# Three late steps of a two-layer pre-norm kernel, moved together: index compares and half of the last norm into the last products, and a low-rank product to the join of h

## The chip, the cores and the metric

One core of one Trainium2 chip. The metric is device time in microseconds (us) for one launch of the whole program; the kernel before took 828.55, 828.6 and 832.93 us in three runs, median 828.6.

## The reference

x is [1024, 512] in fp32 and goes through four residual blocks, each with a layer norm ahead of it: a linear layer under a block mask, an int4 linear layer, an NF4 block with low-rank adapters (q, k, v, o, then gate, up, silu, down with 1792 hidden channels), and a feed-forward in simulated NVFP4. The change touches the end of the third block and the whole of the fourth, which is this:

```python
def nvfp4_qdq(x, select_num):
    s = jnp.maximum(jnp.max(jnp.abs(x)) / (448.0 * 6.0), 1e-12)
    xb = (x / s).reshape(x.shape[:-1] + (D // BLOCK, BLOCK))
    sb = jnp.clip(jnp.max(jnp.abs(xb), axis=-1, keepdims=True) / 6.0, 1e-12, 448.0)
    a = xb / sb
    q = jnp.sign(a) * FP4_LEVELS[jnp.digitize(jnp.abs(a), FP4_BOUNDS)]
    dq = (q * sb).reshape(x.shape) * s
    ...   # the last select_num channels stay as they are
xq = nvfp4_qdq(x2[:, up_reorder_index], SEL_UP)
wg = nvfp4_qdq(w_gate[:, up_reorder_index], SEL_UP)
wu = nvfp4_qdq(w_up[:, up_reorder_index], SEL_UP)
h = jax.nn.silu(xq @ wg.T) * (xq @ wu.T)
hq = nvfp4_qdq(h[:, down_reorder_index], SEL_DOWN)
wd = nvfp4_qdq(w_down[:, down_reorder_index], SEL_DOWN)
out = hq @ wd.T * mlp_output_scale
out = out + x2 @ lr_A @ lr_B
```

The scale s is a maximum over the whole tensor, once of x and once of h (1024 x 1376). So there are two points where nothing that needs the quantised values can begin before everything ahead is done. They are called the join of x and the join of h here.

## The kernel before, in words

Tokens lie on the 128 partitions in 8 tiles of 128 (n = 0 to 7), channels in 4 groups of 128 (k). A product in fp32 precision is three matmuls of 512 columns, high by high, low by high and high by low, at lines 1141, 1142 and 1143 (`pass3`); high and low parts are made by a cast on ACT and a subtraction on DVE or POOL.

`make_plan()` (line 271 on) writes one list of steps with `p.add`. Five functions (`pe_program`, `act_program`, `dve_program`, `pool_program`, `sp_program`) walk this list, and each issues what its engine has to do for a step. So the order of `p.add` is the order on every engine, and an engine that waits holds all its later steps. `p.take` gives a result a bank of PSUM from a ring, with the step that frees it. In the fourth block both rings have four banks (`main4`: banks 0, 1, 2, 7; `turn4`: the other four).

The stages from the end of the third block on, with the steps that the change touches:

- Last products of the third block. Gate/up product and down product for group 6, second token half (`("gu", 6, 1)` with four parts and `("d", 6, 1)` with tiles 4 to 7; the order is set by `order` at line 655). Ahead of `("d", 6, 0)`, four products earlier, stands the step `perm`: SP loads the order of the channels, and DVE turns it to float (L1933) and compares it against the channel numbers in four instructions (L1936). The result is a matrix of zeros and ones by which a product permutes channels. Each down product is added to x on DVE (`dn_add`, L1928). The hidden values of a part come from ACT and, as a product with its high part, from POOL (`gu_mul`).
- Last norm (`norm_turn(3)`, L512): per tile BN_STATS and its kin on DVE, the normed tile `ztok` on ACT, four transposes on PE (`turn`, L1291), the high part from ACT (`tsplit`), the low part from DVE (`tdiff`, L1762). It begins once two down products of the second half have been issued, tile 0 ahead of the last two.
- Permuted product (`pprod`, L1395 on, one matmul pass by the zeros and ones per tile), taken off PSUM by `ptake`. At the same time PE turns weight rows that are gathered by GpSimd in an indirect DMA (`rowfetch`, `rowturn`, `rowsplit`).
- Join of x: `low_a(0)`, `low_a(1)`, the first low-rank product (x by A, 64 wide), around `greatest_of_all("x")`: transposes of the maxima (L1403), a reduce, and a broadcast back (L1407). `low_take` takes x by A off PSUM with ACT (L1608) and DVE (L1962).
- Quantisation of x: `round`, `scale`, `qturn` (transposes, L1437), and between them the hidden product of the first 352 channels, `hidden(0)`, and the second low-rank product: `low_b(n)` for 8 tiles, three matmuls each from 64 partitions, in banks of `main4`, each added to x by DVE (`low_add`, L1967, 8 times). `fetch_pair(1)` turns the next weight rows.
- Hidden products 1 and 2, with `hmm` on PE and silu on ACT. `pair_vacant(1)` (L1205) holds the first load into the buffers of the second pair until `low_b(7)` is done.
- Join of h: `hmax`, `greatest_of_all("h")`: PE transposes the maxima (L1403), DVE reduces, PE broadcasts (L1407), DVE computes the scale (`floor`, `rec`, L2012 on) and rounds the first tile (L2023 to L2036), and PE turns it (L1437).
- Last stage: rounding, turning and the down product of h, tile by tile; `fin` (L2055) adds it to x and the tile goes out.

Of the kernel before, what the change touches and what calls it, by code (L numbers as in the profile page):

```python
# [16 lines left out]
P = 128  # L17
# [27 lines left out]
MASK_LOWS = 2  # L45
MORE_HOTS = 24
# [95 lines left out]
HN = NT // 2  # L142
SCALED_AT = {(0, 0): (0, 1), (0, 2): (1, HN), (HN - 1, 0): (HN, NT)}
# [127 lines left out]
def make_plan():  # L271
# [240 lines left out]
    def norm_turn(ln):  # L512
        norm(ln, 0)
# [6 lines left out]
        for n in range(NT):  # L520
# [132 lines left out]
    norm4, normed = norm_turn(3), 2  # L653
# [39 lines left out]
    for what, g, half in order:  # L693
# [7 lines left out]
        for i, _ in enumerate((gate_up if what == "gu" else down)(g, half)):  # L701
            side_nf4.step()
            side_fp4.step()
            if (what, g, half, i) == ("d", NG - 1, 1, 1):
                next(norm4)
        through.add((what, g, half))
        if (what, g, half) == ("gu", NG - 1, 1):
            next(norm4)
# [7 lines left out]
    def norm4_rest():  # L716
        for n in range(normed):
            yield n
        yield from norm4
        yield None  # L720
        yield None
# [14 lines left out]
    def greatest_of_all(what):  # L736
# [5 lines left out]
        else:  # L742
            p.add("rec", "h", 2, 1)
        p.add("allone", what)
# [8 lines left out]

    for step, _ in enumerate(permuted()):
# [11 lines left out]
    def low_rank():  # L766

        p.add("low_take", 1)
        yield
        for n in range(0, NT + 2, 2):  # L770
            for m in range(n - 2, n):
                if m >= 0:
                    p.add("low_add", m)
            for m in range(n, min(n + 2, NT)):
                p.add("low_b", m)
                main4(("lb", m), ("dve", "low_add", m))
            yield
# [4 lines left out]
    p.add("scale", "x", 0, NT)  # L782

    def turned_tiles(items):
# [50 lines left out]
    first_hidden, low, second = hidden(0), low_rank(), fetch_pair(1)  # L835
    for step, _ in enumerate(turned_tiles([("x", n, 0) for n in range(NT)])):
        if step >= 2:
            next(low, None)
            next(first_hidden, None)
        if step == 3 or step >= 7:  # L840
# [23 lines left out]
    weave(hidden(2), Side(itertools.chain.from_iterable(map(down_rows, range(3))), 1.75))  # L864
    p.add("hmax")
    greatest_of_all("h")
    due = []
# [48 lines left out]
def build(nc, a, out, ctx):  # L916
# [70 lines left out]
    with ExitStack() as late:  # L987
# [8 lines left out]
        w_last = sb("w4_h", [P, 1, 512], F32R, late), sb("w4_l", [P, 1, 512], F32R, late)  # L996

# [24 lines left out]
    lt = [[v[0:LR, 2 + half, :] for v in lrs] for half in range(2)]  # L1022
# [1313 lines left out]
```

## Time and profile before

| | |
|---|---|
| runs | 828.55, 828.6, 832.93 us; median 828.6 |
| profiled execution | 826.45 us, its span 825.0 us |
| granted TensorE clock, mean | 0.958 |
| instructions | 11310 |
| busy PE, DVE, ACT, POOL | 726.9, 570.4, 442.3, 188.5 us |

The profile is of one execution, which was 2.15 us shorter than the median of the three runs. Busy shares are of the whole span. The stages above lie at these times from the start of the span: last products up to 545 us, permuted product up to 572, join of x 572 to 579, quantisation of x and hidden(0) 579 to 650, hidden 1 and 2 up to 732, join of h 732 to 743, last stage 743 to 825. In a row of the timeline the first number is the start, the second the time that the group took; a bracket holds the idle time of the engine ahead of it and what ended it.

### The profile page before, as it was taken

What the parts mean: (1) busy time and instruction counts of PE and PEld (TensorE: products, weight loads), DVE (VectorE), ACT (ScalarE), POOL (GpSimd) and SP (SyncE); (2) the same over time, 40 slices, a digit from 0 to 9 for tenths busy, and PEclk for the clock granted to TensorE, in tenths of its full rate; (3) what the DMA queues carried; (4) which work ended last, traced back from release to release, by engine and by line L of the source; (5) the groups of instructions that cost most, each with busy time, mean ns of one, the idle gap of its engine ahead of it and who ended that gap; (6) DMA issues with size and microseconds to landing.
All of it is one profiled execution on the core that took longest, in us unless ns stands there. A gap on an engine that the chain in (4) does not pass through costs nothing.

```text
span 825.0 us, 11310 instructions
## 1 busy us (share of the span) xinstructions
PE 726.9 (88%) x4136; PEld 540.4 (66%) x4136; DVE 570.4 (69%) x1087; ACT 442.3 (54%) x573; POOL 188.5 (23%) x174
## 2 busy tenths in 40 slices
PE   1898765979999998889998998788899899959998
PEld 1665523656767766557665777566677688957886
DVE  5779967662688778789897985468463433567773
ACT  4778777564876868677766612255422221224542
POOL 1013000004253462435544444112301100000000
PEclk9999968999999999999998999999999999989999
DMA  8636678766376686647655112101301110200001
GB/s 292 213 120 215 198 256 277 254 201 215 129 224 214 201 241 204 236 143 265 232 180 163 65 38 57 42 27 43 99 0 36 36 51 1 87 1 14 25 27 39
DMA packets 56087, 110.55 MB, mean 134 GB/s; under 512 B 9936, under 2 KB 20848, under 8 KB 56032
## 3 DMA queue, kind: packets, MB, share of 16 engines
q1 hardware_dynamic: 42912, 79.22, 29.3%
q10 hardware_dynamic: 8736, 16.52, 6.2%
q0 software_dynamic: 4384, 14.09, 5.6%
q8 instruction: 33, 0.54, 0.3%
q14 instruction: 22, 0.18, 0.1%
HBM read 91.65 MB, written 18.15 MB: 133 GB/s over the span
## 4 chain that ended last, share of the span: by engine, by line
PE 55%; DVE 21%; issue 8%; ACT 8%; DMA 5%; SPq 1%; ACTq 1%; POOL 0%; DVEq 0%; POOLq 0%
PE bank L1141 14%; PE bank L1142 13%; PE bank L1143 13%; PE bank L1249 3%; ACT hot L1551 2%; DVE hot L1805 2%; DMA wide_buf<-in_down_flat 2%; DVE x L1928 2%; PE bank L1437 2%; ACT c L1510 2%; DVE q_a L1878 2%; DVE bank L1831 2%; DVE q_r L1872 1%; PE bank L1291 1%; PE bank L1262 1%
## 5 line engine op out<-in xcount | busy, mean ns | idle before, releaser
L1551 ACT ACTIVATE hot<-rep,levels 128x2048 f16<-128x2048 f16 x96 | 193.6, 2057 | 14.9 <-ACT c L1510 12.1
L1141 PE MATMUL bank<-zt_h,w_h 128*128 128x512 f32 (+1 forms) x232 | 95.1, 410 | 2.6 <-DVE zt_l L1916 2.0
L1142 PE MATMUL bank<-zt_l,w_h 128*128 128x512 f32 (+1 forms) x232 | 92.8, 400 | 0.0
L1143 PE MATMUL bank<-zt_h,w_l 128*128 128x512 f32 (+1 forms) x232 | 92.5, 399 | 0.0
L1249 PE MATMUL bank<-hot,diag 128*32 128x512 f16 x1160 | 78.1, 399 | 2.3 <-ACT hot L1551 2.2
L1141 PE MATMUL bank<-w_h,xq_h 128*128 128x512 f32 (+1 forms) x192 | 74.3, 387 | 5.2 <-DVE w_l L1947 3.0
L1142 PE MATMUL bank<-w_l,xq_h 128*128 128x512 f32 (+1 forms) x192 | 72.3, 376 | 0.0
L1143 PE MATMUL bank<-w_h,xq_l 128*128 128x512 f32 (+1 forms) x192 | 72.2, 376 | 0.0
L2072 POOL TENSOR_TENSOR q_a<-q_a,q_m 128x384 f32<-128x384 f32 (+3 forms) x34 | 35.7, 1049 | 107.9 <-DVE q_m L1691 107.8
L1249 PEld LDWEIGHTS bank<-hot,diag 128*32 128x32 f16 x1160 | 26.1, 98 | 44.9 <-issue 22.8
L2128 POOL TENSOR_TENSOR at_l<-ztok,at_h 128x512 fp32r<-128x512 f32 x28 | 37.5, 1341 | 76.1 <-ACT at_h L1583 76.1
L1141 PE MATMUL bank<-w_h,at_h 128*128 128x512 f32 x112 | 47.9, 427 | 7.2 <-DVE x L1928 5.6
L1141 PEld LDWEIGHTS bank<-zt_h,w_h 128*128 128x128 f32 (+1 forms) x232 | 44.6, 192 | 12.7 <-DVE zt_l L1916 2.4
L2044 DVE TENSOR_TENSOR hid<-hid,bank 128x512 f32<-128x512 f32 (+1 forms) x24 | 15.1, 628 | 53.5 <-PE bank L1143 29.9
L1143 PEld LDWEIGHTS bank<-zt_h,w_l 128*128 128x128 f32 (+1 forms) x232 | 44.6, 192 | 10.5
L1805 DVE TENSOR_SCALAR hot<-rep,levels 128x2048 f16<-128x2048 f16 x58 | 51.0, 879 | 0.1
L1142 PEld LDWEIGHTS bank<-zt_l,w_h 128*128 128x128 f32 (+1 forms) x232 | 44.7, 193 | 9.4
L1583 ACT CAST at_h<-ztok 128x512 fp32r<-128x512 f32 x28 | 17.3, 619 | 60.6 <-DVE ztok L1923 60.6
L1843 DVE TENSOR_TENSOR w_l<-bank,w_h 128x512 fp32r<-128x512 f32 x46 | 31.6, 687 | 24.3 <-ACT w_h L1559 24.0
L1141 PEld LDWEIGHTS bank<-w_h,xq_h 128*128 128x128 f32 x192 | 36.9, 192 | 13.5 <-DVE w_l L1947 3.4
L1142 PE MATMUL bank<-w_l,at_h 128*128 128x512 f32 x112 | 45.4, 405 | 0.0
L1143 PE MATMUL bank<-w_h,at_l 128*128 128x512 f32 x112 | 45.2, 404 | 0.0
(224 smaller groups left out, 1682.7 us busy)
## 6 DMA issues: line engine op xcount, KB each, us to landing
rep<-codes SPq DMA_DIRECT2D x58, 512.0 KB, 4.2
codes<-c SPq DMA_DIRECT2D x28, 256.0 KB
raw<-in_codes_gu_t ACTq DMA_DIRECT2D x14, 512.0 KB, 5.0
sc<-in_scales_gu_t SPq DMA_DIRECT2D x56, 128.0 KB, 4.3
raw<-in_codes_attn_t ACTq DMA_DIRECT2D x8, 512.0 KB, 4.0
raw<-in_codes_down_t ACTq DMA_DIRECT2D x7, 512.0 KB, 5.0
sc<-in_scales_down_t SPq DMA_DIRECT2D x28, 128.0 KB, 3.0
wide_buf<-in_gate_flat SPq DMA_DIRECT2D x5, 512.0 KB, 4.5
```

The costliest lines, as they stand in the source:

```text
L1141: PE.matmul(psum, lh, rh, start=first, stop=False, **kw)
L1142: PE.matmul(psum, lh, rl, start=False, stop=False, **kw)
L1143: return PE.matmul(psum, ll, rh, start=False, stop=last, **kw)
L1249: mm = PE.matmul(bank[32 * q:32 * q + 32, :], lhs, hots[plan.slot[hot_ring(t), (t, m)]][:, q, :], start=m == LOOK_ORDER[0] and part == 0, ...
L1437: last = PE.matmul(bank[0:nr, tok(t)], slot[:, t * P:t * P + nr], ident, start=t == 0, stop=False, is_transpose=True, skip_group_check=True)
L1510: S.copy(c16[:], raw[:]).then_inc(sem("cast_act"), 1)
L1551: S.activation(hots[plan.slot[hot_ring(t), (t, m)]][:], codes_in_place(t), ACT.Relu, bias=bias, scale=slope).then_inc(sem("ramp_act"), 1)
L1583: S.copy(hs[half][0][:, f, :], ztok[plan.slot["ztok", ("silu", *key)]][:]).then_inc(sem("gu_mul_act"), 1)
L1805: ins = V.tensor_scalar(hot, codes_in_place(t), levels[:, HITS:HITS + 1], levels[:, HIT_VALUE:HIT_VALUE + 1], ALU.is_equal, ALU.mult)
L1843: V.tensor_tensor(wl[:, k, :], look_bank(t)[:], wh[:, k, :], ALU.subtract).then_inc(sem("made_dve"), 1)
L2072: G.tensor_tensor(ua[:, 0:nq], ua[:, 0:nq], um[:, 0:nq], ALU.add).then_inc(own.sem, 1)
L2128: G.tensor_tensor(hs[half][1][:, f, :], ztok[plan.slot["ztok", ("silu", *key)]][:], hs[half][0][:, f, :], ALU.subtract).then_inc(sem("gu_m ...
```

## The change

Five things at once, all by moving steps in the plan:

1. The DVE work of `perm` becomes a step `permute` of its own. The loads stay where they were; the cast and the four compares come after the first gate/up part of `("gu", 6, 1)`.
2. The first half of the last norm (tiles 0 to 3) is spread over the eight parts of `("gu", 6, 1)` and `("d", 6, 1)` by `norm4_early`. Tiles 4 to 7 follow after it.
3. The down products of tiles 4, 5 and 6 are cut in two. `dn_ahead` puts their first three matmuls (first 128 of 256 hidden channels) ahead of all of them, and `dn_mm` does the other three.
4. The product `low_b` goes from the quantisation of x to the join of h: tiles 0 and 1 ahead of `greatest_of_all("h")`, 2 and 3 within it, 4 to 7 behind it. Four of its banks come from `turn4`. The addition to x is no longer on DVE: ACT copies the bank to a new buffer `low_sum` and POOL adds it to x. ACT's copies for tiles 6, 7, 4 and 5 stand behind the first rounding of h.
5. `low_take(1)`, and the split of B (a new step `lr_b`, on ACT and POOL), come right after the scale at the join of x, ahead of the first rounding. Their result lies in other buffers, so `pair_vacant(1)` waits for `low_a(1)` only, and `fetch_pair(1)` turns rows from step 5 on instead of step 7.

The core of the diff:

```diff
     def down(g, half):
         for n in range(4 * half, 4 * half + 4):
-            p.add("dn_mm", g, n)
-            p.take("main", 3, ("dn", g, n), ("dve", "dn_add", g, n))
+            if (g, n) in AHEAD:          # AHEAD = (6, 4), (6, 5), (6, 6)
+                if (g, n) == AHEAD[0]:
+                    for ahead in AHEAD:
+                        p.add("dn_ahead", *ahead)
+                        p.take("main", 3, ("dn", *ahead), ("dve", "dn_add", *ahead))
+                p.add("dn_mm", g, n)
...
+    def norm4_early(what, i):
+
+        if (what, i) == ("gu", 0):
+            p.add("permute")
+        elif (what, i) == ("gu", 1):
+            norm(3, 0)
+        elif (what, i) == ("gu", 2):
+            turn_early(0)
+            norm(3, 1)
+        elif (what, i) == ("gu", 3):
+            turn_early(1)
+            split_early(0)
+        elif (what, i) == ("d", 0):
+            split_early(1)
+            norm(3, 2)
+        elif (what, i) == ("d", 1):
+            turn_early(2)
+            norm(3, 3)
+        elif (what, i) == ("d", 2):
+            turn_early(3)
+            split_early(2)
+        else:
+            split_early(3)
...
     p.add("scale", "x", 0, NT)
+    p.add("low_take", 1)
+    p.add("lr_b")
...
-        if step == 3 or step >= 7:
+        if step == 3 or step >= 5:
             next(second)
...
         if c == 1:
-            return [done("pe", "pprod", NT - 1), done("pe", "low_b", NT - 1)]
+            return [done("pe", "low_a", 1)]
...
             p.add("rec", "h", 2, 1)
+            low_b(2, 3)
+            for n in range(4):
+                p.add("low_add", n)
...
                 p.add("round", *item)
+                if item == ("h", 0, 0):
+                    for n in LATER_ADDS:     # 6, 7, 4, 5
+                        p.add("low_add", n)
...
+    low_b(0, 1)
     p.add("hmax")
     greatest_of_all("h")
+    low_b(4, 5, 6, 7)
...
+            elif kind == "dn_ahead":
+                g, n = key
+                half = n // HN
+                bank, (hh, hl), (wh, wl) = main(("dn", *key)), hs[half], wring[2]
+                pe.wait_ge(*done("pool", "gu_mul", g, half, 0))
+                pe.wait_ge(*done("dve", "made", 2 * last_of["down", g] + 1))
+                for m in vacant("main", ("dn", *key)):
+                    pe.wait_ge(*m)
+                k0, tc = 2 * (g % 2), tok(n % HN)
+                pass3(bank[:], hh[:, 0, tc], hl[:, 0, tc], wh[:, k0, :], wl[:, k0, :], True, False)
...
+            elif kind == "low_add":          # ACT
+                n, = key
+                act.wait_ge(*done("pe", "low_b", n))
+                S.copy(low_sum[:, n, :], low_bank(n)[:]).then_inc(sem("low_add_act"), 1)
...
-            elif kind == "low_add":          # DVE
-                n, = key
-                dve.wait_ge(*done("pe", "low_b", n))
-                V.tensor_tensor(x[:, n, :], x[:, n, :], main4(("lb", n))[:], ALU.add).then_inc(sem("low_add_dve"), 1)
...
+            elif kind == "low_add":          # POOL
+                n, = key
+                pool.wait_ge(*done("act", "low_add", n))
+                G.tensor_tensor(x[:, n, :], x[:, n, :], low_sum[:, n, :], ALU.add).then_inc(sem("low_add_pool"), 1)
```

DVE's queue where the index compares stood, before. The rows are line, operation, output and inputs; the first TENSOR_TENSOR adds a down product to x, `hid` here holds the indices, `xq_l` the matrix of zeros and ones.

```order
L1928 TENSOR_TENSOR x<-x,bank2 128x512
L1843 TENSOR_TENSOR w2_l<-bank5,w2_h 128x512
L1933 CAST hid<-hid 128x512
L1936 TENSOR_SCALAR xq_l<-hid,channel 128x512 x4
L1928 TENSOR_TENSOR x<-x,bank0 128x512
L1727 BN_STATS stats<-x 128x6
```

The same place after; the cast and the compares now stand behind the norm's small work, ahead of the first addition to `ztok0`.

```order
L1995 TENSOR_TENSOR x<-x,bank2 128x512
L1910 TENSOR_TENSOR w2_l<-bank5,w2_h 128x512
L1995 TENSOR_TENSOR x<-x,bank0 128x512
L1794 BN_STATS stats<-x 128x6
...
L1822 SCALAR_TENSOR_TENSOR mv<-mv,inv_dev 128x4
L2000 CAST hid<-hid 128x512
L2003 TENSOR_SCALAR xq_l<-hid,channel 128x512 x4
L1990 TENSOR_TENSOR ztok0<-ztok0,bank2 128x512
```

So the additions of group 6 to x no longer stand behind the cast and the compares, and these stand behind the first norm statistics.

DVE's queue at the join of x before: the scales, then at once the first rounding (`q_a0` and `q_a1` are two tiles of it).

```order
L2012 TENSOR_SCALAR rec<-rec,gm4 128x8x24
L2023 TENSOR_TENSOR q_a0<-hid,rec 128x384
L2023 TENSOR_TENSOR q_a1<-hid,rec 128x384
L2030 SCALAR_TENSOR_TENSOR q_a0<-q_m0,q_a0 128x384
```

After, the low part of x by A (`zt_l` from its bank) stands between them.

```order
L2075 TENSOR_SCALAR rec<-rec,gm4 128x8x24
L2029 TENSOR_TENSOR zt_l<-bank1,zt_h 64x512
L2086 TENSOR_TENSOR q_a0<-hid,rec 128x384
L2086 TENSOR_TENSOR q_a1<-hid,rec 128x384
L2093 SCALAR_TENSOR_TENSOR q_a0<-q_m0,q_a0 128x384
```

TensorE's queue at the join of h before: the transpose of the maxima, the broadcast, and the transposes of the first rounded tile (`q_d0`).

```order
L1143 MATMUL bank1<-w1_h,xq_l 128x352
L1403 MATMUL bank3<-ident_r,gm4 1x128
L1407 MATMUL bank3<-ident_r,row 128x1
L1437 MATMUL bank5<-ident_r,q_d0 128x128 x4
```

After, the eight tiles of the second low-rank product, three matmuls each, stand ahead of, between and behind the two.

```order
L1193 MATMUL bank1<-w1_h,xq_l 128x352
L1191 MATMUL bank2<-zt_h 128x512
L1192 MATMUL bank2<-zt_l,zt_h 128x512
L1193 MATMUL bank2<-zt_h,zt_l 128x512
...
L1463 MATMUL bank3<-ident_r,gm4 1x128
L1191 MATMUL bank4<-zt_h 128x512
...
L1467 MATMUL bank3<-ident_r,row 128x1
L1191 MATMUL bank0<-zt_h 128x512
...
L1193 MATMUL bank3<-zt_h,zt_l 128x512
L1497 MATMUL bank4<-ident_r,q_d0 128x128 x4
```

Two tiles lie ahead of the transpose of the maxima, two ahead of the broadcast and four ahead of the first turned tile of h.

## Rows read from the trace of the kernel before

**Rows 1.** The page: busy time, share of the span and instructions of each engine.
```profile
PE 726.9 (88%) x4136; PEld 540.4 (66%) x4136; DVE 570.4 (69%) x1087; ACT 442.3 (54%) x573; POOL 188.5 (23%) x174
```

**Rows 2.** Windows: stretch, length, busy PE, PEld, DVE, ACT, POOL, clock, DMA, GB/s.
```profile
520.00:533.50 13.50, 13.50 (x53) 10.69 (x51) 6.12 (x19) 3.31 (x5) 1.29 (x1) 0.87 0.00 1
533.50:545.60 12.10, 8.94 (x38) 6.83 (x37) 6.08 (x10) 4.51 (x7) 1.27 (x1) 0.86 0.01 1
579.00:650.00 71.00, 65.59 (x295) 51.09 (x295) 35.90 (x60) 21.93 (x44) 10.80 (x12) 0.98 0.15 45
732.00:743.30 11.30, 2.40 (x7) 1.22 (x8) 10.28 (x27) 2.68 (x6) 0.00 (x0) 0.67 0.00 1
```

**Rows 3.** Timeline at the index compares: start, time, engine, line, operation, [idle, releaser].
```profile
516.56 0.43 DVE L1933 CAST hid<-hid 128x512 f32<-128x512 int32 x1 [5.05 <-DMA hid<-in_up_idx]
...
518.61 0.68 DVE L1928 TENSOR_TENSOR x<-x,bank 128x512 f32<-128x512 f32 x1
...
519.35 0.50 PE L1141 MATMUL bank<-w_h,at_h 128*128 128x512 f32 x1 [3.31 <-DVE x L1928]
```

**Rows 4.** Timeline, last down products to the permuted product.
```profile
533.12 0.39 PE L1143 MATMUL bank<-zt_h,w_l 128*128 128x512 f32 x1
...
535.03 1.27 POOL L2128 TENSOR_TENSOR at_l<-ztok,at_h 128x512 fp32r<-128x512 f32 x1 [4.14 <-ACT at_h L1583]
...
543.00 0.39 PE L1143 MATMUL bank<-w_h,at_l 128*128 128x512 f32 x1
...
543.23 0.40 PE L1141 MATMUL bank<-w_h,at_h 128*128 128x512 f32 x1
...
545.54 0.50 PE L1395 MATMUL bank<-xq_l,zt_h 128*128 128x512 f32 x1
...
552.67 0.52 PE L1291 MATMUL bank<-ident_r,ztok 128*128 128x128 f32 x3 [1.83 <-DVE zt_l L1762]
```

**Rows 5.** Timeline at the join of x.
```profile
573.80 1.03 DVE L2023 TENSOR_TENSOR q_a<-hid,rec 128x384 f32<-128x384 f32 x2
...
574.71 0.40 PE L1143 MATMUL bank<-zt_h,w_l 128*64 128x512 f32 x1
...
574.95 0.56 DVE L2030 SCALAR_TENSOR_TENSOR q_a<-q_m,q_a 128x384 f32<-128x384 bf16 x1
...
581.23 0.68 DVE L1962 TENSOR_TENSOR w_l<-bank,w_h 64x512 fp32r<-64x512 f32 x1 [2.30 <-ACT w_h L1608]
```

**Rows 6.** Timeline of the quantisation of x and its end.
```profile
587.33 0.50 PE L1141 MATMUL bank<-w_h 64*128 64x512 f32 x1
...
590.12 0.47 PE L1141 MATMUL bank<-w_h,xq_h 128*128 128x512 f32 x1 [1.14 <-ACT hid L1650]
...
620.98 0.50 PE L1141 MATMUL bank<-w_h,xq_h 128*128 128x512 f32 x1 [0.24 <-ACT xq_l L1636]
...
650.02 0.50 PE L1141 MATMUL bank<-w_h,xq_h 128*128 128x512 f32 x1 [2.95 <-DVE w_l L1947]
...
652.38 0.63 PE L1141 MATMUL bank<-w_h,xq_h 128*128 128x512 f32 x1
...
652.81 0.63 PE L1142 MATMUL bank<-w_l,xq_h 128*128 128x512 f32 x1
```

**Rows 7.** Timeline of PE at the join of h.
```profile
733.55 0.27 PE L1403 MATMUL bank<-ident_r,gm 128*1 128x128 f32 x1 [1.71 <-DVE gm L1978]
...
735.21 0.22 PE L1407 MATMUL bank<-ident_r,row 1*128 1x1 f32 x1 [1.39 <-DVE row L1996]
...
740.29 0.69 PE L1437 MATMUL bank<-ident_r,q_d 128*128 128x128 f32 x2 [4.87 <-DVE q_d L2036]
```

**Rows 8.** POOL and DVE side by side at 505 us, and all of DVE's line 1677.
```profile
505.10 1.29 POOL L2128 TENSOR_TENSOR at_l<-ztok,at_h 128x512 fp32r<-128x512 f32 x1 [3.44 <-ACT at_h L1583]
505.25 1.17 DVE L1677 TENSOR_SCALAR q_r<-q_r 128x14 f32<-128x14 f32 x1
...
L1677 DVE TENSOR_SCALAR q_r<-q_r x34: 174/179/1172, 209.8 to 505.3; 128x24 f32<-128x24 f32 x20, 128x32 f32<-128x32 f32 x8, 128x14 f32<-128x14 f32 x4, 96x24 f32<-96x24 f32 x2
```

More of the change, by code:

```diff
@@ L142 @@
 HN = NT // 2
+AHEAD = tuple((NG - 1, n) for n in range(HN, HN + 3))
 SCALED_AT = {(0, 0): (0, 1), (0, 2): (1, HN), (HN - 1, 0): (HN, NT)}
@@ L510, in norm, with norm_turn @@
         p.take("ztok", 2, ("norm", ln, n), ("pe", "turn", ln, n))
-    def norm_turn(ln):
-        norm(ln, 0)
+    def norm_turn(ln, first=0):
+        if not first:
+            norm(ln, 0)
         if ln == 0:
@@ L519, in norm_turn @@
         turned = None
-        for n in range(NT):
+        for n in range(first, NT):
             p.add("turn", ln, n)
@@ L643, in down @@
         for n in range(4 * half, 4 * half + 4):
-            p.add("dn_mm", g, n)
-            p.take("main", 3, ("dn", g, n), ("dve", "dn_add", g, n))
+            if (g, n) in AHEAD:
[5 more added lines that the diff above has]
+            else:
+                p.add("dn_mm", g, n)
+                p.take("main", 3, ("dn", g, n), ("dve", "dn_add", g, n))
             yield
@@ L651, in down, with turn_early, split_early @@
                     known(3, 0)
-    norm4, normed = norm_turn(3), 2
+    def turn_early(n):
+        p.add("turn", 3, n)
+        turn_bank(("ln", 3, n), split_done(3, n))
+    def split_early(n):
+        p.add("tsplit", 3, n)
+        p.add("tdiff", 3, n)
+    def norm4_early(what, i):
[18 more added lines that the diff above has]
+            split_early(2)
+        else:
+            split_early(3)
     side_nf4, side_fp4 = Side(ready_nf4, NF4_RATE), Side(fp4, FP4_RATE)
@@ L703, in make_plan @@
             side_fp4.step()
-            if (what, g, half, i) == ("d", NG - 1, 1, 1):
-                next(norm4)
+            if (g, half) == (NG - 1, 1):
+                norm4_early(what, i)
         through.add((what, g, half))
-        if (what, g, half) == ("gu", NG - 1, 1):
-            next(norm4)
     p.turn4 = p.turns % 2
@@ L716, in norm4_rest @@
     def norm4_rest():
-        for n in range(normed):
-            yield n
-        yield from norm4
+        yield from range(HN)
+        yield None
+        yield from norm_turn(3, HN)
         yield None
@@ L752, in turn_bank @@
         turn4(key, *freed_by)
+    norm(3, HN)
     for step, _ in enumerate(permuted()):
@@ L764, in low_a, with low_b @@
         main4(("la", half), ("dve", "low_take", half))
[L766 to L777, printed above, removed]
+    def low_b(*tiles):
+        for n in tiles:
+            p.add("low_b", n)
+            (turn4 if n in LOW_IN_TURNS else main4)(("lb", n), ("act", "low_add", n))
     low_a(0)
@@ L833, in hidden @@
         p.note("hup", c, due)
-    first_hidden, low, second = hidden(0), low_rank(), fetch_pair(1)
+    first_hidden, second = hidden(0), fetch_pair(1)
     for step, _ in enumerate(turned_tiles([("x", n, 0) for n in range(NT)])):
         if step >= 2:
-            next(low, None)
             next(first_hidden, None)
-        if step == 3 or step >= 7:
+        if step == 3 or step >= 5:
             next(second)
@@ L996, in build @@
         w_last = sb("w4_h", [P, 1, 512], F32R, late), sb("w4_l", [P, 1, 512], F32R, late)
+    with ExitStack() as end:
+        low_sum = sb("low_sum", [P, NT, D], F32, end)
     wraw = wide_buf[:].rearrange("p (k n) -> p k n", k=KD)
@@ L1021, in build @@
     lrs = w_more
-    lt = [[v[0:LR, 2 + half, :] for v in lrs] for half in range(2)]
+    lt = [[z[0:LR, half * D:half * D + D] for z in zt_flat] for half in range(2)]
+    lr_b = [z[0:LR, 2 * D:3 * D] for z in zt_flat]
     gm4_of = {"x": gm4[:, 0:1], "h": gm4[:, 1:2]}
@@ L1039, in main4, with low_bank @@
         return banks[(0, 1, 2, 7)[plan.slot["main4", key]]]
+    def low_bank(n):
+        return turn(("lb", n)) if n in LOW_IN_TURNS else main4(("lb", n))
     def turn_vacant(key):
@@ L1364, in pe_program @@
                 k0, tc = 2 * (g % 2), tok(n % HN)
-                for k in range(2):
+                for k in range(1 if key in AHEAD else 0, 2):
                     last = pass3(bank[:], hh[:, k, tc], hl[:, k, tc], wh[:, k0 + k, :], wl[:, k0 + k, :], k == 0,
```

36 lines of the change are left out of this document (22 added, 14 removed).

## The prediction

> **What bounds the kernel now.** I read the page first: PE is busy 88% of the span and no other engine is above 69% [rows 1]. So a change can win by taking PE's idle time or slow clock, and hardly by taking work from DVE, ACT or POOL. Then I read windows over the stages that the change touches, for PE's busy time and clock [rows 2]. PE is packed in the x quantisation (65.59 of 71.00 us). At the join of h it works 2.40 of 11.30 us while DVE works 10.28, so DVE bounds there. In the two stretches around the last products the clock is 0.87 and 0.86, where the page's mean is 0.958. Last I read the timeline at each PE gap for what ends it [rows 3 to 7]. Sums are made against the profiled execution, 826.45 us (span 825.0); that run was 2.15 under the median of 828.6, and I add this back at the end.
>
> One price first. Products are issued one matmul after the other: 543.00 to 543.23 is 0.23 us a matmul at the full clock of 2.4 GHz [rows 4], and 652.38 to 652.81 is 0.43 at the lower level of 1.2 GHz [rows 6].
>
> **A, the index compares leave the first-half down products.** DVE waits 5.05 us for the indices, until 516.56; the cast, the compares and one addition follow, and PE stands 3.31 us for that addition [rows 3]. After the move nothing on DVE waits for the indices at this place, and at the new place, some 10 us later, they have landed. PE gets back 3.3. After the gap the stretch up to 533.5 runs at clock 0.87 [rows 2]: 13.50 us x 0.13 = 1.75 lost, which I read as the price of the pause and count as won. A = -5.1 (bounds -3.3, if the clock dips anyway, and -5.1).
>
> **B, last norm and split products.** The last gate/up matmul starts at 533.12, the first permuted one at 545.54 [rows 4]: 12.4 us, in which PE is busy 8.94 of 12.10 [rows 2]. The largest pause is for POOL's product of hidden values (535.03 + 1.27 = 536.30, after 4.14 us without work) [rows 4]. After the change this stretch holds a turn (0.55), nine matmuls ahead (9 x 0.23 = 2.1) that need only the first half of the hidden values, a wait for the rest, 15 more matmuls (3.5) and two to three turns (1.4); with the wait at 0.5 that is 8.1. B = 8.1 - 12.4 = -4.3, of which 0.2 is uncertain either way. If DVE or ACT cannot serve norm and hidden values at once, half is lost: bounds -2 and -5.
>
> **C, permuted product.** The gap of 1.83 for the low part of a turned tile [rows 4] goes, since tiles 0 to 3 are ready; the same engines make tiles 4 to 7 in the same time, so I let new waits of 0.7 appear. C = -1.1 (bounds 0 and -1.8).
>
> **D, join of x.** Now DVE goes from the scales straight to the first rounding at 573.80, while PE still does `low_a(1)` until 574.71 + 0.40 = 575.11 [rows 5]. After the change DVE first takes x by A off PSUM, which waits for that product and ACT's copy (0.6, an estimate from the 0.56 and 0.68 of the rows beside it), and takes 0.68 itself [rows 5]: 575.11 + 0.6 + 0.68 - 573.80 = +2.6 ahead of everything that waits for the first rounding. Beside that, POOL's subtraction for B runs at the same moment as DVE's first rounding. What that does, the trace has elsewhere: at 505.25 a DVE instruction of 14 columns takes 1.17 us where the median of its line is 179 ns, while POOL works from 505.10 to 506.39 [rows 8]: it ends as POOL ends. So I add 1.1. D = +3.7 (bounds +2.6, +4.0).
>
> The Trainium skill has the rule for this (SBUF — State Buffer, "Who interferes with whom"): the two engines share ports by a lock that blocks the second to ask, for instructions with two SBUF inputs and in fast modes; the trace agrees, with 1.17 us against 179 ns. By the rule D is +3.7, and without it +2.6; it speaks against F below too.
>
> **E, quantisation of x.** 24 matmuls of `low_b` leave a stage where PE is packed [rows 2]; one stands at 587.33 [rows 6]. 24 x 0.233 = 5.6. The products before and after them wait little now, and some waits that they covered come up, as the 0.24 at 620.98 [rows 6]; I take four of 0.3, +1.2. The gap of 1.14 at 590.12 goes, as the additions to x leave DVE. The last gap of 2.95 at 650.02 stands ahead of the second hidden product, which waits for weight rows that DVE has split [rows 6]; these now start two steps earlier, and I count it all. After it the clock falls, 652.38 on, for about 4 us: 0.20 more a matmul, 1.4 to 1.8. Sum: -5.6 + 1.2 - 1.1 - 3.0 - 1.5 = -10.0 (bounds: -4.4 if nothing but the matmuls comes, -11.5 without new waits).
>
> **F, join of h.** PE has three gaps there, 1.71, 1.39 and 4.87 [rows 7], together 8.0, and the 24 matmuls need 5.6 at full clock, so they fit; the window's clock is 0.67 [rows 2], and at 0.43 a matmul 24 take 10.3. The first two tiles stand ahead of the transpose of the maxima, 1.4 to 2.6, against a gap of 1.71; so up to 0.9 late. ACT's copies fit in its 8.6 us idle. What does not fit is POOL. DVE bounds the join with short operations on SBUF; no POOL work is there now (0.00) [rows 2]. Eight additions with two SBUF inputs come, each about the 1.29 of the POOL row at 505.10 [rows 8]: 10.3 us in two batches of four. If every DVE instruction gets its turn only between two of POOL's, the first batch is in series: 4 x 1.29 = 5.2. Of the second, DVE is one tile ahead and PE has products queued, so I take half less 0.8: 1.8. F = +7.0 (bounds: -1 if POOL does not disturb and the slow clock ends earlier, +11.6 if all eight and one more wait are in series).
>
> **Sum.** -5.1 - 4.3 - 1.1 + 3.7 - 10.0 + 7.0 = -9.8. 826.45 - 9.8 = 816.65 profiled; with 2.15, 818.8.
>
> **Rivals.**
>
> R1: POOL hardly disturbs DVE, because most instructions of the join are small or read PSUM. For it: of the 34 instructions of that DVE line the median stays at 179 ns, so most met no harm. Against it: the one that fell on POOL's work took 1.17 us [rows 8]. Then F = 0 and D = +2.6: 826.45 - 5.1 - 4.3 - 1.1 + 2.6 - 10.0 = 808.55, with 2.15 810.7. Chance 0.15.
>
> R2: the early parts win half. PE's gaps are moved, not filled: in B, ACT and DVE, which have their queues in a fixed order, do the norm ahead of hidden values, and in E the stage turns from PE to the loop of rounding, turning and splitting. For it: DVE works 35.90 us and ACT 21.93 of 71.00 there [rows 2], with long dependent chains. Against it: PE is packed 92%, so little of the loop shows. Then B, C, E give -2.2, -0.5, -5.0: 826.45 - 5.1 - 7.7 + 3.7 + 7.0 = 824.35, with 2.15 826.5. Chance 0.15.
>
> R3, slower: the low clock outlives the join of h. The join grows by 7 and is emptier in part, the clock there is 0.67 [rows 2], and a matmul at the lower level costs 0.20 more [rows 6]. Each us of the last stage at 1.2 GHz loses half a us. If it stays for 28 us, 14 are lost: 818.8 + 14 = 832.8. It decides from about 20 us (10 lost, all the gain). For it: after the pauses at 519 and 650 the clock dips [rows 2, 6]. Against it: after the gap at 650.02 it was low for about 4 us only, and the low-rank product now keeps PE busier in the join. Chance 0.05.
>
> R4: the change does not do what it says: the first tiles of `low_b` at the low clock delay the maxima by up to 2.3 and everything of the join behind them. That is 818.8 + 2.3 = 821.1, inside my range; chance 0.1.
>
> **How the numbers follow.** Forecast 818.8, chance 0.55; its own range 815 to 823. R1 0.15, R2 0.15, R4 0.10, R3 0.05. To hold 8 in 10 the range goes down to 808.5, which leaves out the far side of R1, and up to 826.5, the middle of R2, which leaves out R3 and half of R2. What a measurement can tell from no change is 0.5%, 4.1 us: faster is under 824.5, slower over 832.7. Faster: forecast, R1, R4 and a third of R2, 0.85. Same: the rest of R2, 0.10. Slower: R3, 0.05.
>
> **What the new profile would show.** A: no PE gap by an addition to x in the first-half products, clock over 0.95 there. B: the first permuted matmul 4 us sooner after the last gate/up one than 12.4. D: the first rounding about 2.6 us later behind the scales, with one subtraction of DVE in between, and the first rounding above its usual 1.03 for two. E: no `low_b` between 579 and 650, the stage 8 to 10 us shorter, gaps under 1 ahead of the second hidden product. F: eight POOL additions at the join, DVE's rounding instructions over 1 us each where they were 0.5, and the first turned tile of h 5 us later behind the maxima. If those instructions keep their time, my F is wrong and the time is near 811; if PE waits as long as before in the x stage, R2 holds.

## The result: less than half of the gain that was forecast

| | before | after |
|---|---|---|
| runs, median | 828.55 to 832.93, 830.15 us (8 runs) | 824.32 to 826.47, 825.64 us (8 runs) |
| profiled execution | 826.45 us | 826.44 us |
| span, mean clock | 825.0 us, 0.958 | 825.0 us, 0.948 |

The ratio is 0.994 (95% interval 0.9927 to 0.9954), a gain of 4.5 us by the medians. The forecast was 818.8 with -9.8: the time lies inside the range of 808.5 to 826.5, but the gain is less than half of the one forecast.

The two profiled executions show no difference at all, and that is the first thing to clear up. In both, PE does the same matmuls up to the gap at 519 us. The 2731st of them starts at 502.05 before and at 506.42 after, though nothing that the change touches lies ahead of it. Over all profiles of this study that start lies between 500.67 and 510.75 us, in code that is the same. Much of this goes with the chip: it is 505.12 to 506.87 in the four experiments on chip 4, 507.21 to 510.75 on chip 13 and 500.67 to 504.51 on chip 7. (For the two kernels here the chip is not on record.) The profiled execution of before was faster than all eight timed runs. From that matmul on the two profiles differ by -4.4, which is what the medians show.

So every profile is read from that matmul on, in stages whose borders are starts of matmuls in PE's timeline: the last one of the gate/up product (533.12 before), the first permuted one (545.54), the transpose of the maxima of x (570.99), the first turned tile of x (576.75), the last hidden matmul (731.52), the fifth transpose of h (743.30), and the end. The stages are the steps A to F of the prediction, with A ending at the gate/up product.

| change of each stage, us | A | B | C | D | E | F | rest | sum |
|---|---|---|---|---|---|---|---|---|
| forecast | -5.1 | -4.3 | -1.1 | +3.7 | -10.0 | +7.0 | 0 | -9.8 |
| after | -4.7 | -4.5 | +5.6 | +3.4 | -10.9 | +5.9 | +0.7 | -4.4 |

Five of six terms are within 1.1 us. C missed by 6.7.

The profile after. The page's busy times stand as those of before do in [rows 1]: PE as before, POOL 11 us more.

```profile
PE 728.5 (88%) x4136; PEld 541.1 (66%) x4136; DVE 572.7 (69%) x1079; ACT 447.7 (54%) x581; POOL 199.9 (24%) x182
```

Windows of after, columns as in [rows 2]: the permuted stage, the quantisation of x, the join of h.

```profile
540.70:571.76 31.06, 26.15 (x125) 20.79 (x125) 19.68 (x42) 15.14 (x27) 5.49 (x6) 0.89 0.16 43
580.97:644.96 63.99, 61.05 (x277) 47.76 (x277) 30.10 (x52) 22.59 (x46) 12.34 (x13) 0.96 0.19 55
726.89:745.00 18.11, 11.76 (x33) 8.13 (x34) 17.08 (x27) 7.73 (x15) 10.66 (x8) 0.58 0.00 1
```

The permuted stage took 25.45 us before (545.54 to 570.99) and takes 31.06 now. PE is busy for 26.15 of it and stands for the other 4.9 us, in two gaps of 1.40 and 3.50. The join of h has 10.66 us of POOL where it had none, and DVE is busy 17.08 of 18.11.

**Where C went.** Timeline of PE in the permuted stage of after. L1341 is the turn of a normed tile, L1445 that of weight rows, L1455 the permuted product.

```profile
550.00 0.60 PE L1341 MATMUL bank<-ident_r,ztok 128*128 128x128 f32 x4
552.01 0.66 PE L1341 MATMUL bank<-ident_r,ztok 128*128 128x128 f32 x4 [1.40 <-ACT ztok L1581]
552.50 0.60 PE L1445 MATMUL bank<-ident_r,hid 128*128 128x128 f32 x4
556.60 1.09 PE L1341 MATMUL bank<-ident_r,ztok 128*128 128x128 f32 x4 [3.50 <-DVE w_l L2014]
557.34 0.78 PE L1455 MATMUL bank<-xq_l,zt_h 128*128 128x512 f32 x1
557.92 0.63 PE L1456 MATMUL bank<-xq_l,zt_l 128*128 128x512 f32 x1
```

Tiles 4 and 5 are turned, then PE stands 3.50 us for a bank of PSUM that DVE's split of weight rows (L2014) frees. Behind the waiting turn of tile 6 stands the permuted product of tile 4 (L1455 and L1456). DVE in the same stretch:

```profile
553.16 0.69 DVE L1829 TENSOR_TENSOR zt_l<-bank,zt_h 128x512 fp32r<-128x512 f32 x1 [0.95 <-ACT zt_h L1588]
553.77 0.68 DVE L2020 TENSOR_REDUCE blk<-bank 128x32 f32<-128x512 f32 x1
...
554.73 0.75 DVE L1742 RECIPROCAL rec<-rec 128x96 f32<-128x96 f32 x1
...
555.77 0.69 DVE L2014 TENSOR_TENSOR w_l<-bank,w_h 128x512 fp32r<-128x512 f32 x1
```

The low part of tile 4 (L1829) is there at 553.85, 2.75 us before PE moves on. The product had its inputs; it was queued behind a turn that could not run. Before the change the first-half products filled this time. Now they are done by 550, and nothing covers the second half's chain. It starts on ACT:

```profile
544.35 1.28 ACT L1574 ACT_TABLE_LOAD   x1 [4.47 <-DVE mv L1806]
...
547.22 0.82 ACT L1581 ACTIVATE ztok<-x,mv,inv_dev 128x512 f32<-128x512 f32 x1 [1.36 <-DVE mv L1822]
547.94 0.57 ACT L1671 COPY hid<-bank 128x512 f32<-128x512 f32 x1
```

ACT waits 4.47 us for the statistics, with the takes of permuted tiles (L1671) behind. I first took this for the main cause. After the gap the granted clock is at its lower level (a permuted matmul 0.63 us long where 0.40 is usual, as at 557.92) until 562.4. So the +5.6 can be taken apart: 4.90 us of gaps where before had 1.83, +3.1; from 556.60 to 562.4 PE works at the lower level, 5.8 us, by an estimate from 0.43 a matmul against 0.23 about +2.8; one turn fewer lies in the stage, about -0.35.

**D and F.** At the join of x in after, first the wait that was forecast, then POOL and DVE side by side:

```profile
575.46 0.40 PE L1193 MATMUL bank<-zt_h,w_l 128*64 128x512 f32 x1
575.89 0.58 ACT L1675 CAST zt_h<-bank 64x512 fp32r<-64x512 f32 x1 [3.35 <-PE bank L1193]
...
576.57 0.68 DVE L2029 TENSOR_TENSOR zt_l<-bank,zt_h 64x512 fp32r<-64x512 f32 x1 [2.06 <-ACT zt_h L1675]
577.07 1.78 POOL L2201 TENSOR_TENSOR zt_l<-hid,zt_h 64x512 fp32r<-64x512 f32 x1 [22.74 <-ACT zt_h L1653]
577.18 2.08 DVE L2086 TENSOR_TENSOR q_a<-hid,rec 128x384 f32<-128x384 f32 x2
```

The two multiplications took 1.03 before [rows 5] and take 2.08. The join of h, POOL and DVE, in after:

```profile
727.72 0.43 DVE L1744 TENSOR_SCALAR rec<-rec 128x88 f32<-128x88 f32 x1
...
728.50 0.91 DVE L2059 COPY row<-row 1x127 f32<-1x127 f32 x1
...
730.49 1.37 DVE L2074 TENSOR_SCALAR blk<-blk,gm 128x86 f32<-128x86 f32 x1
...
734.45 5.76 POOL L2205 TENSOR_TENSOR x<-x,low_sum 128x512 f32<-128x512 f32 x4 [2.67 <-ACT low_sum L1657]
734.90 1.63 DVE L2099 TENSOR_TENSOR q_d<-q_a,blk 128x512 f32<-128x512 f32 x1
736.46 1.36 DVE L2074 TENSOR_SCALAR blk<-blk,gm 128x258 f32<-128x258 f32 x1
737.74 1.35 DVE L2075 TENSOR_SCALAR rec<-rec,gm 128x258 f32<-128x258 f32 x1
739.13 1.33 DVE L2086 TENSOR_TENSOR q_a<-hid,rec 128x224 f32<-128x224 f32 x1
```

POOL's four additions of the row run from 734.45 to 740.22, the second batch. The four DVE instructions that start in that time take 0.9 to 1.0 us longer than in a kernel that has no additions there (f_held, below), 258 columns as much as 512. The first batch runs from 726.77 to 731.79, and there not every DVE instruction is late: the COPY, L1744 and L2074 are, but four instructions of one column between 729.72 and 730.45 take their usual 0.15 to 0.16, and a reciprocal of 88 columns its 0.70. Between the two batches, from 731.8 to 734.45, DVE keeps its pace.

### The profile page after: what moved, and what is told of

It reads as the page before. It is cut to its first block, busy times and chain, and to the rows that moved or that the text cites. A ratio compares the mean times of both kernels' runs of the same rounds, so it can differ in the third digit from the quotient of the medians.

```text
span 825.0 us, 11312 instructions
## 1 busy us (share of the span) xinstructions
PE 728.5 (88%) x4136; PEld 541.1 (66%) x4136; DVE 572.7 (69%) x1079; ACT 447.7 (54%) x581; POOL 199.9 (24%) x182
## 4 chain that ended last, share of the span: by engine, by line
PE 53%; DVE 20%; ACT 10%; issue 9%; DMA 4%; SPq 1%; another core or an unknown queue 1%; ACTq 1%; POOL 0%; DVEq 0%; POOLq 0%
PE bank L1191 13%; PE bank L1192 13%; PE bank L1193 13%; PE bank L1299 3%; ACT hot L1611 3%; DMA wide_buf<-in_down_flat 2%; DVE x L1995 2%; DVE hot L1872 2%; ACT c L1570 2%; DVE bank L1898 2%; PE bank L1497 2%; DVE q_a L1945 1%; PE bank L1312 1%; PE bank L1341 1%; DVE q_r L1939 1%
## 5 line engine op out<-in xcount | busy, mean ns | idle before, releaser
L1193 PEld LDWEIGHTS bank<-zt_h,w_l 128*128 128x128 f32 (+1 forms) x232 | 43.9, 189 | 10.3
L1191 PE MATMUL bank<-w_h,zt_h 128*128 128x512 f32 (+1 forms) x104 | 43.5, 418 | 0.0
```

What stands on the lines that cost most here:

```text
L1191: PE.matmul(psum, lh, rh, start=first, stop=False, **kw)
L1193: return PE.matmul(psum, ll, rh, start=False, stop=last, **kw)
```

## The experiments

Each was timed beside runs of the kernel before on the same chip. Chips differ between rows: chip 4 (before 831.21 us) has a_compares, c_half_late, c_norm_at2 and f_no_adds; chip 13 (832.61) has f_held, d_later, c_product_first and g_all; chip 7 (827.07) has the rest. So ratios are compared, not times, and two ratios that differ by under 0.3% are not told apart. The table has the ratio, and the stages as above of the one profile of each kernel, against the profile of before.

| kernel | ratio (95%) | A | B | C | D | E | F | sum |
|---|---|---|---|---|---|---|---|---|
| a_compares | 0.9966 (0.9953 to 0.9979) | -5.2 | +1.0 | 0.0 | 0.0 | +0.1 | 0.0 | -3.9 |
| c_half_late | 0.9948 (0.9929 to 0.9967) | -5.2 | +1.1 | 0.0 | +3.5 | -10.5 | +6.1 | -4.3 |
| after | 0.994 (0.9927 to 0.9954) | -4.7 | -4.5 | +5.6 | +3.4 | -10.9 | +5.9 | -4.4 |
| c_norm_at2 | 0.994 (0.992 to 0.9959) | -4.7 | -4.5 | +3.2 | +3.6 | -9.7 | +6.0 | -4.9 |
| c_first_only | 0.9909 (0.988 to 0.9938) | -4.7 | -4.5 | +1.0 | +3.6 | -10.3 | +5.9 | -8.0 |
| c_product_first | 0.9886 (0.9861 to 0.9911) | -4.7 | -4.5 | -0.2 | +3.6 | -9.7 | +6.0 | -8.3 |
| f_no_adds | 0.9876 (0.9856 to 0.9896) | -4.7 | -4.5 | +4.1 | +3.6 | -10.1 | +0.1 | -10.9 |
| f_held | 0.9889 (0.986 to 0.9918) | -4.7 | -4.5 | +4.1 | +3.6 | -10.1 | +0.1 | -10.9 |
| d_later | 0.9874 (0.9845 to 0.9903) | -4.7 | -4.5 | +5.7 | 0.0 | -9.5 | +6.0 | -6.9 |
| d_split_later | 0.9946 (0.9924 to 0.9968) | -4.7 | -4.5 | +4.2 | +2.6 | -9.6 | +6.0 | -4.7 |
| e_fetch7 | 1.0004 (0.9979 to 1.0029) | -4.7 | -4.5 | +4.2 | +3.6 | -5.4 | +5.9 | -0.4 |
| g_half_late | 0.9832 (0.9805 to 0.9859) | -5.2 | +1.1 | 0.0 | 0.0 | -10.9 | +0.1 | -14.4 |
| g_all | 0.9778 (0.9753 to 0.9803) | -4.7 | -4.5 | -0.2 | 0.0 | -9.4 | +0.1 | -18.1 |

The sum holds the rest up to the end too, at most 1.3. Sum and ratio agree within 2 us, save for d_later. E lies between -9.4 and -10.9 in all kernels that turn the weight rows early, without order by what was changed, so differences of E under 1.5 are not read.

**a_compares**

```diff
-            p.add("perm")
...
+            if (what, g, half, i) == ("gu", NG - 1, 1, 0):
+                p.add("perm")
```

> The kernel before with part 1 of the change alone: the cast and the four compares of the indices stand behind the first gate/up part of the second half. Theory (parts add up; the profile after shows 5.2 us for this part): 830.15 - 5.2 = 825 us, ratio 0.994. Rival (the clock dip behind the gap comes anyway, only the 3.3 us of the gap are won): 827 us, ratio 0.996.

Measured 828.29 against 831.21, -2.8 us by the ratio. The stage wins 5.2, and 1.0 comes back in B, where the clock was low for 6.8 us (from 533.9) and in the profile before for 3.4. The two other kernels with the compares moved and the late norm, c_half_late and g_half_late, have 6.8 there too. That is three profiles against one, so that the longer dip belongs to the change is likely and not shown. The time fits the rival (827 of 830.15, a ratio of 0.996), though for another reason than it gave: the dip behind the old gap is gone.

**c_half_late**

```diff
-AHEAD = tuple((NG - 1, n) for n in range(HN, HN + 3))
+AHEAD = ()
...
-            if (g, half) == (NG - 1, 1):
-                norm4_early(what, i)
+            if (what, g, half, i) == ("gu", NG - 1, 1, 0):
+                p.add("permute")
+            if (what, g, half, i) == ("d", NG - 1, 1, 1):
+                next(norm4)
...
```

> The kernel after with parts 2 and 3 undone: the last norm's first half and the down products of tiles 4 to 6 stand as before. Theory (the early half wins 4.0 up to the first permuted product and loses 5.6 in the permuted stage, since ACT's takes stand behind the second half's statistics): 1.6 us faster than after, about 824, and in its trace no gap over 2 us of PE in the permuted stage. Rival (the loss in the permuted stage has another cause, such as the gathers or a chance dip of the clock): 4 us slower than after, about 829.5.

Measured 0.9948 where after has 0.994: the same. C falls from +5.6 to 0.0 and B rises from -4.5 to +1.1. So parts 2 and 3 as they stand bring nothing. The theory's 1.6 us faster did not come: by the ratios it is 0.7 slower, by the stages the same. The rival's 4 us slower is excluded.

**c_norm_at2**

```diff
-    norm(3, HN)
     for step, _ in enumerate(permuted()):
+        if step == 2:
+            norm(3, HN)
```

> The kernel after with the second half's statistics and its first normed tile issued after the take of permuted tile 0, not ahead of all takes. Theory (ACT's order is the cause: the takes wait behind the statistics, then ACT has 8.6 us of work at a stretch and PE runs dry): the PE gaps of 1.40 and 3.50 us in the permuted stage shrink by 1.2 to 2.5 together, and the clock dip after them may go; 1.5 to 5 us faster than after, 821 to 824. Rival (gathers or the chain of the second half itself decide): same as after within 0.5 us, or slower by what the statistics are late, 0.5 to 1 us.

Measured 0.994, as after: the time is the rival's. The gap of 1.40 is gone, so the two gaps shrink by 1.2 together, but the other stays, in its PE timeline:

```profile
555.85 0.66 PE L1342 MATMUL bank<-ident_r,ztok 128*128 128x128 f32 x4 [3.69 <-DVE w_l L2015]
```

C is +3.2, where the six kernels with after's order have 4.1 to 5.7. So ACT's order is the small part of the loss. That it was the main cause, my first theory of C, fell here.

**c_product_first and c_first_only.** The first has the statistics' move too, the second only this (`next(rest, "end")` issues the next turn):

```diff
-        for n in norm4_rest():
-            if turned is not None:
+        rest = norm4_rest()
+        while True:
+            early = turned is not None and turned >= HN
+            if early:
+                p.add("pprod", turned)
+                main4(("p", turned), ("dve", "ptake", turned))
+            n = next(rest, "end")
+            if n == "end":
+                return
+            if turned is not None and not early:
                 p.add("pprod", turned)
```

> The kernel after with the statistics of the second half behind the take of tile 0, and, for tiles 4 to 7, the permuted product issued on PE ahead of the next turn and not behind it. Theory (PE stands 3.5 to 3.7 us for a bank, with the permuted product of tile 4 ready but queued behind the turn of tile 6): the gap falls under 1.5 us, the permuted stage is 2 to 4 us shorter than with the statistics moved alone, whose step from the first permuted product to the maxima was 3.2 us longer than before; the time is 2 to 5 us below after, 821 to 823.5. Rival (ACT and DVE are the bound of this stretch, whatever PE's order): the gap moves to the next turn or product and the time is that of after within 1 us.

> The kernel after with PE's order alone changed: for tiles 4 to 7 the permuted product ahead of the next turn; the second half's statistics still ahead of all takes. Theory A (the queued product is the main cause of the 5.6 us, ACT's order a small one): from the first permuted product to the maxima 1 to 1.5 us longer than before, against 4.1 to 5.7 in after and -0.2 with both cures. Theory B (both are needed, as ACT's backlog decides): 3 us or more longer than before.

Measured 0.9886 with both and 0.9909 with this alone; C is -0.2 and +1.0. The timeline of PE in c_first_only (L1463 is the permuted product, L1349 the turn):

```profile
548.72 0.50 PE L1463 MATMUL bank<-xq_l,zt_h 128*128 128x512 f32 x1 [0.81 <-DVE zt_l L1837]
...
551.41 0.63 PE L1349 MATMUL bank<-ident_r,ztok 128*128 128x128 f32 x4 [0.57 <-DVE w_l L2022]
```

The gap of 3.50 has become 0.81 and 0.57 with a product between them, and the clock stays up through the stage. PE's order is the main cause of the miss: 3.1 to 4.7 us of C, of which 2.1 are idle time and the rest goes with the dip of the clock; the order of ACT is another 1.2. Theory A's 1 to 1.5 came out at 1.0, and theory B's 3 or more is excluded. The statistics moved alone (c_norm_at2) take 0.9 to 2.5 off C and nothing off the time.

**f_no_adds and f_held**

```diff
-                G.tensor_tensor(x[:, n, :], x[:, n, :], low_sum[:, n, :], ALU.add).then_inc(sem("low_add_pool"), 1)
+                G.tensor_tensor(low_sum[:, n, 0:1], x[:, n, 0:1], low_sum[:, n, 0:1], ALU.add).then_inc(sem("low_add_pool"), 1)
```

```diff
...
-            elif kind == "low_add":
+            elif kind == "low_sum":
                 n, = key
                 pool.wait_ge(*done("act", "low_add", n))
-                G.tensor_tensor(x[:, n, :], x[:, n, :], low_sum[:, n, :], ALU.add).then_inc(sem("low_add_pool"), 1)
+                pool.wait_ge(*done("pe", "qturn", "h", n, 0 if n else 2))
+                G.tensor_tensor(x[:, n, :], x[:, n, :], low_sum[:, n, :], ALU.add).then_inc(sem("low_sum_pool"), 1)
...
```

The first diff is f_no_adds, the second f_held: there the addition becomes a step of its own, `low_sum`, added to the plan behind the copies, and waits for a transpose of the last stage.

> The kernel after with POOL's eight additions of the low-rank product at the join of h cut to one column each, so the low-rank part is left out of the output. Theory (POOL's additions hold up DVE's short operations at the join): DVE's L2074, L2075, L2086 and L2099 keep their usual 0.3 to 0.7 us there, and the time is 6 to 7 us below after, about 819. Rival (the low-rank matmuls at the low clock, or ACT's copies, delay the join): as after, 825.6, the first turned tile of h as late behind the maxima.

> The kernel after with all of POOL's eight additions kept, but each held back until the last stage: tile 0 until the third piece of tile 0 of h is turned, tile n until the first piece of tile n is. ACT's copies stay at the join. Theory (POOL's additions cost the join 5.9 to 6.6 us, and in the last stage PE bounds and DVE has slack): 5 to 6 us below after, 820 to 821; the join as in the kernel without additions. Rival (a DVE instruction held up by POOL is late for PE in the last stage as well, since the rounding chain is the limit there too): 0 to 2 us below after.

Measured 0.9876 and 0.9889, by the ratios 5.3 and 4.2 us below after, with the same F of +0.1 and sums of -10.9. So all of F was POOL's additions, and in the last stage all eight are free to within the noise. They still hold DVE there: a rounding step at 746.46 takes 1.67 where its neighbours take 0.69, but PE, which has products queued, is not late. DVE at the join in f_held:

```profile
730.11 0.21 DVE L2061 COPY row<-row 1x127 f32<-1x127 f32 x1
...
731.53 0.27 DVE L2076 TENSOR_SCALAR blk<-blk,gm 128x86 f32<-128x86 f32 x1
...
734.85 0.69 DVE L2101 TENSOR_TENSOR q_d<-q_a,blk 128x512 f32<-128x512 f32 x1
735.46 0.35 DVE L2076 TENSOR_SCALAR blk<-blk,gm 128x258 f32<-128x258 f32 x1
735.73 0.35 DVE L2077 TENSOR_SCALAR rec<-rec,gm 128x258 f32<-128x258 f32 x1
736.11 0.39 DVE L2088 TENSOR_TENSOR q_a<-hid,rec 128x224 f32<-128x224 f32 x1
```

The same six took 0.91, 1.37, 1.63, 1.36, 1.35 and 1.33 in after; L1744's 0.43 is 0.21 here. Added up, DVE loses 2.0 us beside the first batch and 3.9 beside the second, together the 5.9 of F. POOL's own time is unchanged in size, 10.7 us for eight:

```profile
L2208 POOL TENSOR_TENSOR x<-x,low_sum 128x512 f32<-128x512 f32 x8 | 10.7, 1335 | 150.8 <-PE bank L1499 150.8
```

**d_later and d_split_later.** Both steps, or `lr_b` alone, issued at step 2 of the quantisation:

```diff
-    p.add("low_take", 1)
-    p.add("lr_b")
...
+        if step == 2:
+            p.add("low_take", 1)
+            p.add("lr_b")
```

> The kernel after with the taking of x by A (second half) and the split of B not ahead of the first rounding of x, but two roundings later. Theory (D as measured, 3.45 us: 2.4 of waiting for PE and ACT in DVE's order, 1.05 of POOL beside the first rounding): the first turned tile of x comes 3.4 us sooner behind the maxima than in after, and the time is 2.5 to 3.5 below after, 822 to 823. Rival (the quantisation of x is bounded by something that starts independently, such as the gathered rows): first turned tile sooner, but the start of hidden product 1 within 0.5 us of after, and so the time.

> The kernel after with the split of B alone (ACT's cast and POOL's subtraction) issued two roundings later; x by A is still taken ahead of the first rounding. Theory (3.45 us is 2.4 of DVE's wait and 1.05 of POOL beside the first rounding): the first two rounding multiplications take 1.03 us and not 2.08, the first turned tile of x comes 1.0 us sooner behind the maxima, with 2.4 left. Rival (the wait is all of it, and DVE only waits longer): 0.3 us sooner or less.

D is 0.0 and +2.6, against +3.4 to +3.6: 1.0 for POOL, 2.6 for the order of DVE, as forecast. In d_split_later the two multiplications take 1.01 again:

```profile
570.44 0.68 DVE L2030 TENSOR_TENSOR zt_l<-bank,zt_h 64x512 fp32r<-64x512 f32 x1 [2.06 <-ACT zt_h L1676]
571.05 1.01 DVE L2087 TENSOR_TENSOR q_a<-hid,rec 128x384 f32<-128x384 f32 x2
```

In the time less can be seen: d_split_later is 0.9946, as after, and 1.0 us is below what these ratios tell apart. In d_later E holds a new gap of PE, 1.50 at 601.03, so part of the 3.4 is given back; g_all, with the same step moved, has 0.53 there and g_half_late none over 0.5. The six runs of d_later spread over 10 us (818.15 to 828.26), so its ratio is weak evidence; its stages are better.

**e_fetch7**

```diff
-        if step == 3 or step >= 5:
+        if step == 3 or step >= 7:
```

> The kernel after with the turning of the second pair of weight rows from step 7 of the quantisation of x again, not from step 5. Theory (the gap of 2.95 us ahead of hidden product 1 goes by the two earlier steps): the gap comes back, 2 to 3 us, with a dip of the clock, +3 to +4 us from the first turned tile of x to the middle of hidden 1 and 2, about 829 us. Rival (the gap went since the rows no longer wait for the low-rank product): within 1 us of after.

Measured 1.0004, no faster than before. In its timeline the gap of 2.95 [rows 6] is back, within 0.01:

```profile
641.87 0.50 PE L1191 MATMUL bank<-w_h,xq_h 128*128 128x512 f32 x1 [2.96 <-DVE w_l L2014]
```

In after the row reads:

```profile
644.96 0.50 PE L1191 MATMUL bank<-w_h,xq_h 128*128 128x512 f32 x1 [0.26 <-DVE w_l L2014]
```

E is -5.4, where the other kernels with the early rows have -9.4 to -10.9: one number in one condition is worth 4.0 to 5.5 us with the clock dip (low for 3.4 us from 642.5), somewhat over the theory's 3 to 4. The rival is excluded. Freeing the load from the low-rank product is worth nothing alone; whether the early rows would pay without it was not run. The -5.4 that is left is the moved product, and F's +5.9 takes all of it. So without the early rows the five-part change wins nothing.

**g_half_late and g_all.** g_all has the cures of f_held, d_later and c_product_first; g_half_late has the first two, with parts 2 and 3 of the change undone.

> The version with the additions held and x by A taken later, but the last norm's first half and the down products as before, that is with parts 2 and 3 of the change undone. Theory (parts 2 and 3 win 5 us once their permuted stage is mended and nothing before): steps of A, E and F as in the version with all cures, 819 us, 5 us above it (814.2). Rival (the mended early half wins little, and the 814.2 come from the two other cures): 815 to 816.

> The three cures together: additions held to the last stage, x by A taken later, statistics behind the first take and products ahead of turns. Theory (all three losses are separate stretches, so the gains add): -5.9 - 3.4 - 3 = 12 us below after, 813.5. Rival (the second stage of a gain is eaten by the clock or the next limit): 816 to 819.

g_all measures 814.16 us (812.99 to 814.84) against 832.61, ratio 0.9778; that beats both kernels, and the gain is about 18 us where the change alone brings 4.5. The gains add, as the theory had it (813.5); the rival's 816 to 819 is excluded. g_half_late is 0.9832, so parts 2 and 3, once mended, are worth the difference of the ratios, 0.54% or 4.5 us, near the theory's 5. By the stages it is 5.3 in A to C and 3.8 in all, as E differs by 1.5 the other way. The two ratios are of different chips, and with their intervals the 4.5 can be 1.5 to 7.5. Parts 2 and 3 were never separated from each other.

## Why the prediction was wrong, step by step

- **A**, forecast -5.1: -5.2 alone, and -4.7 in after, where a turn of the early norm lies in it. The clock's share was booked as won; in a_compares 1.0 comes back in a longer dip at the next pause.
- **B**, forecast -4.3: -4.5. The gap for POOL's product of hidden values is 0.34 in after. My reading of the pause before was half right. These rows of before show that PE's two gaps there end with normed tiles from ACT; POOL's product is done between them, at 536.30. Both waits are gone in after.

```profile
535.73 0.66 PE L1291 MATMUL bank<-ident_r,ztok 128*128 128x128 f32 x4 [2.22 <-ACT ztok L1521]
537.26 0.65 PE L1291 MATMUL bank<-ident_r,ztok 128*128 128x128 f32 x4 [0.88 <-ACT ztok L1521]
```

- **C**, forecast -1.1: +5.6, and 4.1 to 5.7 in the six profiles with this order. This is the step that failed: the new waits, put at 0.7, measured 4.90, and the clock was low behind them, for which C had no term. It said that "the same engines make tiles 4 to 7 in the same time, so I let new waits of 0.7 appear". I had counted that the gap of 1.83 [rows 4] goes, and not asked what covered the chain of the second half: the first-half products. With B they had moved ahead, PE was out of work at 550, and its next instruction was one that needed a bank from DVE. The bounds (0 and -1.8) did not hold the result either, as no upper bound was worked out from the length of the stage. c_first_only and c_product_first show the cause.
- **D**, forecast +3.7: +3.4 to +3.6, of it 2.6 the wait and 1.0 POOL (d_split_later), for which I had 2.6 and 1.1.
- **E**, forecast -10.0: -10.9. The weight rows' earlier start is 4.0 to 5.5 of it (e_fetch7), for which I had 4.5, and the rest is the -5.4 of e_fetch7, for which I had -5.5.
- **F**, forecast +7.0: +5.9. The cause was right, the split between the batches was not: 3.0 before the first turned tile and 3.0 behind it, for 5.2 and 1.8. By batch it is 2.0 for the first and 3.9 for the second. The first was taken as fully in series, but it ends at 731.8, before the rounding of the first tile, and several DVE instructions beside it are not late at all; the second meets that tile's last step and the beginning of the next. Rival R1 (POOL hardly disturbs) is excluded by f_no_adds.
- R2 foresaw half the gain, but by B, C and E all winning half. B and E won in full; what it had right is that a gap is moved and not filled, in C alone. That the time came out near its 826.5 is chance.
- R3 did not come: the clock is low until 746.8 in after, 4.2 us into the last stage, not 28. Nor did R4: from the last hidden matmul to the transpose of the maxima it is 2.03 us in both profiles.
- The base: the profile before was 3.7 us below the median of eight runs, and 2.15 was added back for three. This changes the predicted time and not the difference. The time lies in the range since the range went up to the middle of R2; for C it is no support.

## What to carry to other kernels

Work that is moved out of a stage may have been cover for a chain there. After every such move, ask what the engine does at that moment instead, and whether the next instruction in its queue is one that can run; a ready product behind a blocked turn cost most of what the move had won (3.1 to 4.7 of 5.3). An engine with hardly any work is no free place if its work holds up a neighbour that is the limit: hold the work back until a stage in which the neighbour has slack. And compare profiles stage by stage from a common instruction, since a difference in the early part, of the execution or of the chip, can hide the whole effect.

## What the runs showed of the hardware

- While POOL adds two SBUF tiles, five DVE instructions of 86 to 512 columns on SBUF take 1.33 to 1.63 us, where 0.27 to 0.69 is theirs (after against f_held). A reciprocal of 88 columns (0.70) and four instructions of one column (0.15 to 0.16) take no longer beside it.
- The hold goes the other way too: POOL's subtraction beside DVE's first rounding took 1.78 in after and c_half_late, and 1.27 alone (d_split_later). In the six other kernels with this order it took 1.25 to 1.26, and DVE's first multiplication was the one held (1.55 to 1.56 against 0.54); in the two it was the second. Who is first varies between executions, and D with it only from 3.45 to 3.61. The Trainium skill (SBUF — State Buffer, "Who interferes with whom") says that the first to issue has the pair for its whole instruction; these durations agree.
- After the same gap of PE the granted clock was low for 3.4 us in four profiles (C +4.1 or +4.2) and 6.8 in two (C +5.6 or +5.7). That is 1.5 us between executions of one code, and a term with a clock dip should carry it.
- From the join of h on the clock is low for 17.1 us in after and 6.8 us in f_held. Both stretches end 4.0 to 4.2 us behind the fifth transpose of h, and the last stage takes the same within 0.1 us; so the longer dip costs that stage nothing.
